# Adding the returned expert outputs onto h: from GpSimd and VectorE to VectorE alone

## The reference

```python
h = tokens_embedded(x)                                # [16, 256, 128]
h = h + attention(layernorm(h))
xf = layernorm(h).reshape(4096, 128)
gates = softmax(xf @ Wg + bg)                         # 8 experts
vals, idx = top_k(gates, 2); vals = vals / (vals.sum() + 0.01)
hid = relu(xf @ W1[e] + b1[e])                        # 128 -> 512, for each chosen expert e
y   = hid @ W2[e] + b2[e]                             # 512 -> 128
out = h + sum over the token's two experts of vals * y
```

## Time and profile before

| | |
|---|---|
| median of three runs | 375.48 us (375.06 to 375.69) |
| the profiled execution | 372.63 us |
| its span, first to last instruction | 370.9 us |
| PE busy / DVE / ACT / POOL | 90% / 85% / 68% / 60% of the span |
| DMA | 29.81 MB in 33242 packets |

### The profile page before, as it was taken

How to read it: one execution, slowest core, us unless ns; L and a number is a source line. 1 busy time by engine, 2 the same in 40 slices (tenths; PEclk the granted TensorE clock), 3 DMA queues, 4 the chain that set the end, 5 groups by cost and what they waited for, 6 DMA issues and landing times.

```text
span 370.9 us, 11470 instructions
## 1 busy us (share of the span) xinstructions
PE 334.5 (90%) x2986; PEld 290.1 (78%) x2986; DVE 313.4 (85%) x1203; ACT 252.8 (68%) x670; POOL 222.8 (60%) x421
## 2 busy tenths in 40 slices
PE   7958999999999999999997899986999999999830
PEld 3526888888878787787876899986999999999820
DVE  7687999999989999999997679989987777789942
ACT  1645888789877788888875667764677777766620
POOL 6000310777786777877776777876655554667750
PEclk9985999999999999999999999999999999999985
DMA  6075720000101000010102122322332222256466
GB/s 160 23 210 151 216 66 2 19 26 24 35 34 34 25 27 17 31 32 32 32 34 58 42 80 84 94 84 73 103 102 85 78 68 75 78 158 193 158 178 198
DMA packets 33242, 29.81 MB, mean 80 GB/s; under 512 B 4749, under 2 KB 27624, under 8 KB 33192
## 3 DMA queue, kind: packets, MB, share of 16 engines
q1 hardware_dynamic: 25832, 17.91, 17.4%
q0 software_dynamic: 4352, 9.45, 7.6%
q10 hardware_dynamic: 3008, 1.89, 1.7%
HBM read 16.50 MB, written 12.73 MB: 79 GB/s over the span
## 4 chain that ended last, share of the span: by engine, by line
PE 78%; DVE 8%; issue 5%; DMA 3%; ACT 2%; POOL 1%; SPq 1%; ACTq 0%; DVEq 0%; POOLq 0%
PE ps_oy L1721 9%; PE ps_out L1711 9%; PE ps_vc L1721 8%; PE ps_out L1614 8%; PE ps_q L1711 7%; PE ps_oy L1631 7%; PE ps_vc L1604 4%; PE ps_qT L1596 3%; PE ps_oy L1624 3%; PE ps_k L1562 2%; PE ps_qT L1703 2%; PE ps_k L1711 2%; PE ps_vc L1585 2%; PE ps_vc L1586 2%; PE ps_vc L1587 2%
## 5 line engine op out<-in xcount | busy, mean ns | idle before, releaser
L740 POOL DMA_INDIRECT y_dram<-heads_out,place x72 | 74.8, 1038 | 46.7 <-ACT heads_out L928 35.3
L719 POOL DMA_INDIRECT slots_dram<-rows,row_id x64 | 63.7, 996 | 18.4 <-issue 17.6
L919 ACT ACTIVATE k_prime<-ps_out,b_T 128x128 f32<-128x128 f32 x108 | 32.1, 365 | 19.6 <-PE ps_out L1711 19.6
L919 ACT ACTIVATE k_prime<-ps_q,b_T 128x128 f32<-128x128 f32 x108 | 31.8, 365 | 16.7 <-PE ps_q L1711 16.6
L1417 DVE COPY w_tile<-w_all 128x640 f32 x72 | 41.8, 581 | 1.2
L1721 PE MATMUL ps_oy<-w_tile,k_prime 128*128 128x128 f32 x288 | 38.6, 277 | 4.0 <-issue 3.1
L1711 PE MATMUL ps_out<-sT,w_tile 128*128 128x128 f32 x288 | 38.5, 276 | 1.6 <-issue 1.4
L1721 PEld LDWEIGHTS ps_oy<-w_tile,k_prime 128*128 128x128 f32 x288 | 35.0, 192 | 5.0 <-issue 4.7
L1721 PE MATMUL ps_vc<-w_tile,k_prime 128*128 128x128 f32 x288 | 38.3, 276 | 0.2 <-issue 0.2
L684 POOL TENSOR_TENSOR rstd<-moments,ln_eps 128x4 f32<-128x4 f32 (+1 forms) x19 | 3.8, 200 | 57.0 <-DVE moments L1040 55.2
L1711 PEld LDWEIGHTS ps_out<-sT,w_tile 128*128 128x128 f32 x288 | 35.0, 192 | 2.6 <-issue 2.6
(11 more groups left out here) (267 smaller groups left out, 884.4 us busy)
## 6 DMA issues: line engine op xcount, KB each, us to landing
qkv_rows<-slots_dram SPq DMA_DIRECT2D x72, 72.0 KB
y_sum<-y_dram SPq DMA_DIRECT2D x14, 256.0 KB, 3.4
w_all<-in_L_ffn_W SPq DMA_DIRECT2D x1, 2048.0 KB, 13.7
w_all<-in_L_ffn_W SPq DMA_DIRECT2D x8, 256.0 KB, 4.6
out<-h SPq DMA_DIRECT2D x6, 256.0 KB, 3.4
y_dram<-heads_out,place POOLq DMA_INDIRECT x72
slots_dram<-rows,row_id POOLq DMA_INDIRECT x64, 2.3
qkv_rows<-in_L_attn_w_qkv ACTq DMA_DIRECT2D x1, 768.0 KB, 6.2
```

What stands on the lines that cost most here:

```text
L719: nc.gpsimd.indirect_dma_start(slots_dram[:, :], bass.IndirectOffsetOnAxis(row_id[:, place_of(p, a), j, k:k + 1], 0), rows[:, place_of(p, ...
L740: nc.gpsimd.indirect_dma_start(y_dram[:, :], bass.IndirectOffsetOnAxis(place[:, a, :], 0), y[:, a, :], None).then_inc(s_placed[a], 16)
L919: last = nc.scalar.activation(hT[:, a % 2, c, :], ps_up[a % 2][0][:, c * P:c * P + P], ACT.Relu, bias=b1_T[:, bass.ds(experts[0] * FC + c, ...
```

## The change

POOL's additions (add_both) and VectorE's add_sum are dropped. In their place VectorE adds each half of a chunk onto h itself (add_y(c, k), k = 0 for the first and 1 for the second expert): chunks 0 and 1 behind slot tiles 61, 64, 67 and 70, one half at a time; chunks 2 to 5 behind the last slot tile, in the order (2,0) (3,0) (2,1) (3,1) (4,0) (5,0) (4,1) (5,1). SP writes only chunks 0 and 1 ahead of its last reads, and chunks 2 to 5 behind them. The reads of the chunks stay where they are.

```diff
+        SUM_FROM, SUM_EVERY = SUMMED_BY + 5, 3
...
-        s_both, s_sum = sem("both_y_added"), sem("y_added_to_h")
+        s_first, s_sum = sem("first_y_added_to_h"), sem("both_y_added_to_h")
... SP
-            for c in range(Y_SUMS - 1):
+            for c in range(Y_LAST):
                 write_summed(sp, c)
             read_last(sp, 0)
-            write_summed(sp, Y_SUMS - 1)
+            for c in range(Y_LAST, Y_SUMS):
+                write_summed(sp, c)
             write_last(sp, 1)
... POOL, place_y
-                if isinstance(n, int) and n % 2 == 0:
-                    add_both((n - SUMMED_BY) // 2 - 1)
-            def add_both(c):
-                if not live(c, Y_SUMS):
-                    return
-                pool.wait_ge(s_read[c], 16 * TOP)
-                at = slice(c * Y_TILES, c * Y_TILES + Y_TILES)
-                nc.gpsimd.tensor_tensor(y_sum[:, 0, at, :], y_sum[:, 0, at, :], y_sum[:, 1, at, :], ALU.add)\
-                    .then_inc(s_both, 1)
... VectorE, slot_tile
-                if isinstance(n, int) and n % 2 == 1:
-                    add_sum((n - SUMMED_BY - 1) // 2 - 3)
-            def add_sum(c):
-                if not live(c, Y_SUMS):
-                    return
-                dve.wait_ge(s_both, c + 1)
+                if isinstance(n, int) and n >= SUM_FROM and (n - SUM_FROM) % SUM_EVERY == 0:
+                    add = (n - SUM_FROM) // SUM_EVERY
+                    if add < TOP * Y_LAST:
+                        add_y(add // TOP, add % TOP)
+            def add_y(c, k):
+                if k == 0:
+                    dve.wait_ge(s_read[c], 16 * TOP)
+                else:
+                    dve.wait_ge(s_first, c + 1)
                 at = slice(c * Y_TILES, c * Y_TILES + Y_TILES)
-                nc.vector.tensor_tensor(h[:, at, :], h[:, at, :], y_sum[:, 0, at, :], ALU.add).then_inc(s_sum, 1)
+                nc.vector.tensor_tensor(h[:, at, :], h[:, at, :], y_sum[:, k, at, :], ALU.add)\
+                    .then_inc(s_first if k == 0 else s_sum, 1)
... VectorE, behind the slot tiles
+            for c in range(Y_LAST, Y_SUMS, 2):
+                for k in range(TOP):
+                    add_y(c, k)
+                    add_y(c + 1, k)
```

## The result

The first comparison gave 370.5 us (median of four, 369.28 to 371.88) against 375.59 before, a ratio of 0.9893 (95% interval 0.9852 to 0.9934). A second comparison with more runs (12 of the changed kernel, 23 of the one before) gave 371.29 against 374.49, ratio **0.9919** (0.9892 to 0.9946): 3.0 us less. The ratios on record are taken over the fast runs and are not quotients of the medians: 370.5 / 375.59 would be 0.9864.

What follows compares the result with a forecast made beforehand. TensorE held 78% of the chain of waits, its pace lost in the last tiles. Pace (3.11 us) and POOL's queue (0.84) gain 3.95, the tail costs 1.18: -2.77, from 375.48 to 372.7 us, range 371.0 to 374.7.

Steps and rivals of the forecast that it cites:

- Pace: Last expert tiles: without POOL's additions VectorE's copies lose their long form and TensorE regains 3.11 us, bounds 0 to 3.11.
- Four additions among the tiles: VectorE's additions behind tiles 61, 64, 67 and 70: cost 0, or 0.9 us without cover.
- the cover of 1.2 us: Among the last tiles: VectorE can be about 1.2 us late without TensorE losing time.
- POOL's queue: Last scatters on POOL: without its additions the last one starts 0.84 us earlier, beyond the returned pace.
- rival C: Behind the last tile: the train of additions holds POOL's last scatters, +2.3 us, 377.8 us; chance 6%.
- Landing: From the last scatter's start to SP's read: kept at 2.68 us, possibly a few tenths less.
- Tail: From SP's last reads to the end: three more writes make it 1.18 us longer, between 0 and 2.3.
- rival B: In the tail: the writes slow the last reads, the last landing 8.5 us after issue; -1.15 us, 374.3 us; chance 12%.
- Rival A: In the tail: the writes cost nothing, -3.95 us, 371.5 us; chance 22%.
- D: Last expert tiles: the pace doesn't return, as the reads of y cause the loss; +0.34 us, 375.8 us; chance 4%.

Runs made afterwards that it cites:

- e1: The kernel before without GpSimd's six additions, the second half left out of the output of 24 token tiles; ratio 0.9899 to the kernel before.
- e2: The changed kernel with six GpSimd additions of the same size put back at the old places, into a buffer nobody reads; ratio 1.0050 to the kernel before.
- e9: The changed kernel with all twelve additions among the tiles, only chunk 5 written behind the last reads; ratio 0.9857 to the kernel before.
- e5: The changed kernel with eight additions among the tiles, chunks 0 to 3 written between the tiles; ratio 0.9881 to the kernel before.
- e3: The changed kernel with all twelve additions behind the last slot tile, chunks 0 and 1 first; ratio 0.9920 to the kernel before.
- e10: The changed kernel without SP's writes of chunks 3, 4 and 5; one profiled run, 37.54 us from tile 61's up product to the span's end.
- e7: The changed kernel with eight more VectorE copies right behind the last bias add; one profiled run, 38.40 us from tile 61's up product to the span's end.
- e4: The changed kernel with SP's writes of chunks 2 and 3 issued ahead of the last reads; ratio 0.9898 to the kernel before.
- e6: The changed kernel with six GpSimd memsets at the old additions' places; one profiled run, 38.11 us from tile 61's up product to the span's end.

## Why the prediction was right

In terms of L the gain is 3.07 us for a forecast of 2.77. The mechanism was right; that the sum is so close owes something to errors of both signs: +0.10 in the pace, -0.25 in POOL's queue, +0.32 in the landing, +0.13 in the tail.

*Pace, 3.11 predicted, 3.21 measured.* The mechanism is shown from both sides (e1, e2). The pace just before the additions held to the end; the 0.1 more is the last step, 3.68 us instead of 3.79. Before, two tiles took up to 4.75 us (TensorE's timeline):

```profile
342.27 1.13 PE L1711 MATMUL ps_out<-sT,w_tile 128*128 128x128 f32 x8 [0.22 <-issue]
...
347.02 1.13 PE L1711 MATMUL ps_out<-sT,w_tile 128*128 128x128 f32 x8 [0.56 <-issue]
```

*Four additions among the tiles, 0 predicted, 0 measured.* Zero, four, eight, ten and twelve of them leave tile 71 at +18.85 or +18.84. The zero was right, but these runs don't reach the cover of 1.2 us from which it was argued. In e9 VectorE's relu block starts 1.22 us behind the up product of its tile while undisturbed, 1.42 behind it after the first addition, and never more than 1.61. So the first addition makes VectorE 0.20 us late (0.22 predicted), and each further one, tile after tile, only 0.025: VectorE then takes 1.92 us a tile (345.50, 347.42, 349.34) where TensorE takes 1.895. The 0.15 a tile of e5's expectation was too much.

*POOL's queue, 0.84 predicted, 0.59 measured* (28.66 - 24.86 less 3.21). The scatter of tile 69 starts 3.21 behind the up product of tile 71, not 3.06, and the last two steps take 1.27 and 1.53, 2.80 instead of 2.7. The additions beside them are the reason for the second: without a train (e1, e9) both steps are 1.26 to 1.27 and the last scatter starts at +24.59. This is what is left of rival C: 0.27 us, in some runs 0.55 more behind the last scatter's start (1.50 instead of 0.95 in e3 and e10), where C needed 2.77. The starts and ends show what C had right: a scatter waits for a VectorE addition or copy with all its operands in SBUF that runs across its start, and ends 0.8 to 0.9 us behind it. In the changed kernel the addition from 355.01 to 355.70 runs across the start of the scatter at 355.30, which ends at 356.53. But the scatter doesn't wait for the additions queued behind that one. Where an addition and the last scatter start within 0.03 us of each other, one of the two is held. In the changed kernel it is the addition (0.74 us, the scatter 0.95), in e10 the scatter (1.50, the addition 0.69). VectorE of the changed kernel, then VectorE and POOL of e10:

```profile
356.82 0.74 DVE L1431 TENSOR_TENSOR h<-h,y_sum 128x512 f32<-128x512 f32 x1
```

```profile
355.89 0.69 DVE L1430 TENSOR_TENSOR h<-h,y_sum 128x512 f32<-128x512 f32 x1
```

```profile
355.92 1.50 POOL L741 DMA_INDIRECT y_dram<-heads_out,place  x1 [0.30 <-issue]
```

The row that the prediction used against C (337.63) has an addition that starts inside the scatter. The row that bears on it is the scatter at 355.54, 1.25 us, with the long addition from 354.20 to 355.94 across its start.

The Trainium skill, "SBUF — State Buffer", section "Who interferes with whom", gives VectorE's copies and GpSimd's instructions one port pair under a lock. For the long copies the traces agree (1.93, 2.23, and 1.16 beside a memset). The Trainium skill, on the same page under "SBUF: two separate sides", has a software-descriptor DMA beside a VectorE copy go from 620 ns to about 3100. These traces don't show that price: it is 0.12 us a scatter under copies (e7), 0.27 to 0.54 under additions. The prediction held it against a train of additions, which that passage doesn't speak of.

*Landing, kept at 2.68, measured 2.36.* The prediction said that it could be a few tenths less, with the queued writes gone, and it was. e1, e3 and e4 show the same dependence from the other side: with writes issued shortly before the last scatter it is 3.3. By the packets of POOL's queue, the last scatter's data are in 0.90 us behind its end in the changed kernel, e9 and e10, but 1.21 before, 1.31 in e3, 1.84 in e4 and 1.87 in e1, and SP's read follows half a microsecond later in each.

*Tail, 1.18 predicted, 1.05 measured.* The term is right, and its size in part by errors that cancel. From the second total to the last packet it took 4.21 us (1.38 MB by the packets), where the prediction put 4.66: the writes went at 344 to 348 GB/s, not at 281, an estimate from a stretch in which scatters were mixed in. The reads were in 0.28 us later than before (5.96 instead of 5.68, a small part of rival B). From the last packet at 369.37 to the end of the span it took 0.75, where 0.7 was taken from between 0 and 1.8. e10 shows that the term itself is the writes: without three of them the tail is 9.78.

Rival A (the writes cost nothing) and rival B in full (the last read 8.5 us after its issue) are both refuted by these numbers, C by e7 and by the changed kernel itself, D by e1.

## What to carry to other kernels

Before work is given to an idle GpSimd, look at what VectorE copies between SBUF buffers at that time: a GpSimd instruction of 1.28 us cost VectorE 1.1 to 1.7 us each time that it met such a copy (1.93 against 0.42, 2.23 against 0.49), and TensorE lost up to 0.96 us in two tiles by it (4.75 instead of 3.79, from 342.27 to 347.02 before). How late an engine may be before the bottleneck feels it, can be estimated from one disturbed instruction: its excess less what the bottleneck lost. What a piece of added work costs an engine is read from its period with the work in it (1.92 us in e9), not from the work's length. And at the end of a kernel writes set ahead of the last dependence delayed its landing by what they saved behind it (e4); moving them into the stretch of the tiles, where the DMA engines were 66% to 75% busy from 330 to 350 us, gained (e9).

## What the runs showed of the hardware that was not expected

- A GpSimd memset, which reads nothing, stretches a VectorE copy too: 1.16 us beside a memset of 0.54 (e6), where the same copy takes 0.56 in the changed kernel.
- A scatter is held by the VectorE addition or copy between SBUF buffers that runs across its start, and ends 0.8 to 0.9 us behind that one: 350.91 behind an addition's end at 350.02 (e9, 1.42 us), 354.60 behind a copy's end at 353.78 (e7, 1.08 us). Alone it takes 0.96. The longer addition therefore costs it more than the copy. A relu block, which reads PSUM, across its start doesn't hold it (0.96 us at 352.10 in the changed kernel, the relu from 352.05 to 352.40). Some scatters among the tiles are longer for another reason, which is not worked out here (1.65 us at 346.41).
- The granted clock after the same pause of TensorE differs from one execution to the next (0.79 in the changed kernel's profile and in e1's, 1.00 in the profile before and in the changed kernel's second one, over 256 to 264 us). With the drop behind 200 us it came with an up product of tile 61 that was 2.27 us later. The spans of the two profiles alone would have hidden most of this change.
